# In the mixer's last tile, VectorE instead of GpSimd makes the low parts and the square sums

## The chip, the cores and the metric

The kernel runs on one core of one Trainium2 chip. The metric is the time of one execution on the device in microseconds; of several runs the median counts. Engines are named as the profile names them: PE is TensorE's matmuls, PEld its weight loads, DVE is VectorE, ACT is ScalarE, POOL is GpSimd, SP issues the DMA transfers. "Granted clock" is TensorE's clock as a share of 2.4 GHz; 0.50 is 1.2 GHz.

## The reference, cut to what matters

Eight sequences of 256 tokens with 256 features go through a layer norm. Its result feeds a state-space mixer and a six-block MLP, and the output is the input plus both results. The mixer:

```python
zxbcdt = hidden_states @ W_in
z, xbc, dt = ...
xbc = _causal_conv1d(xbc, conv_w, conv_b)
x, Bm, Cm = ...
dt = jax.nn.softplus(dt + dt_bias)
y = _ssd(x, dt, A, Bm, Cm, CHUNK)
y = y + D[None, None, :, None] * x
yg = y * _silu(z)
rms = jax.lax.rsqrt(jnp.mean(yg * yg, axis=-1, keepdims=True) + EPS)
yn = (yg * rms) * norm_w
return yn @ W_out
```

Two parts of it matter here: the gated result `yg`, which is multiplied by `W_out`, and the mean of its squares over all 4096 inner features.

## The kernel before, in words

The program has three phases with a barrier of all engines between them: `prepare` (layer norm, the projections of B, C and dt, decay sums), `mix` (the mixer) and `mlp` (the six blocks). All 2048 tokens stay in SBUF.

`mix` goes over the 4096 inner features in `NCT` = 32 tiles of 128 features (c = 0 to 31), and in each tile over `NB` = 4 blocks of 512 tokens (b = 0 to 3; two sequences s to a block). Matrix products are made in split precision: an operand is cut into a high part (a cast to fp32r on ScalarE) and a low part (operand minus high part), and three products are added. For the gated result of a tile and block the chain is:

1. VectorE makes the decay exponents (`exponents`, L989), ScalarE their exponential (`decays`, L874), GpSimd multiplies by masked C.B (`times_g`, L681), and TensorE multiplies with the tokens (`outputs`, L769) into one of two PSUM tensors `py`.
2. VectorE adds D.x (`add_dx`, L1004) and gates with silu(z) into `yg` (`gate`, L1017).
3. ScalarE squares it (`square`, L883) and casts the high part `ghi` (`high`, L919). GpSimd makes the low part `glo` (`low`, L670) and adds the square to the running sum `sqacc` (`add_square`, L690).
4. After every second tile TensorE multiplies the pair's `ghi` and `glo` with two tiles of `W_out` (`output_rows`, L787 to L789): eight groups of 12 matmuls, two groups to a block (i = 0, 1), each into one of two PSUM banks `po[i]`. VectorE adds each group to `acc` (`add_rows`, L1030), which frees the bank.

The order on each engine is written out by hand in its `step(c)`, which runs for c = -2 to 34 and is fully unrolled. One step works on several tiles at once: in step c GpSimd makes the products of tile c and the low parts and squares of tile c - 1. Engines run their lists in order, and semaphores that count upwards join them. The end of the mixer is step 32, where no tile of exponents is left, and the rest of the output rows in steps 33 and 34. In this text m0 to m7 are the eight groups of output rows of the last pair of tiles: m0 to m3 of step 32, m4 to m7 of step 33.

Group m waits until the addition of group m - 2 has emptied its bank:

```python
wait_past(pe, o_added, 2 * NB * q + 2 * b + i - 1)
```

On VectorE the end of the mixer is, in order: `gate` of block 2, `add_dx` of block 3, `add_rows` of the pair before, `add_rows` of m0, `gate` of block 3, `add_rows` of m1 to m7. On ScalarE `high` of blocks 2 and 3 stands behind `square` of block 3. After the output rows TensorE sums `sqacc` over the features with 16 one-column products (L822), VectorE makes the mean square from them (L1069), and the barrier ends the phase.

At the start of the mixer VectorE fills a PSUM tensor `floor` with a constant (L972); only its first column is read, by `exponents`, as a broadcast operand.

Of the kernel before, what the change touches and what calls it, by code (L numbers as in the profile page):

```python
# [23 lines left out]
F32 = mybir.dt.float32  # L24
F32R = mybir.dt.float32r
ALU = mybir.AluOpType
# [10 lines left out]
NCT = DI // P  # L37
PAIRS = NCT // 2
# [5 lines left out]
NB = TOK // BLK  # L44
TPB = BLK // P
SPB = BLK // SEQ
# [6 lines left out]
CAP = 80.0  # L53
# [468 lines left out]
def wait_past(eng, sem, count):  # L522

    if not (isinstance(count, int) and count <= 0):
        eng.wait_ge(sem, count)
# [6 lines left out]
def mix(nc, w_xz, conv_par, d_par, w_out, w1, cs_dram, ident, xhi, xlo, acc, gmat, tokpar,  # L532
        wraw, whi, wlo, w_in, conv, conv_in, srow, srow_in, xt, zt, stages, w1raw, w1_in, meansq):

    DVE_G = [(0, 0)]
    POOL_G = [(b, s) for b in range(NB) for s in range(SPB) if (b, s) not in DVE_G]

    with ExitStack() as ctx:
        sb = lambda name, shape, dt=F32: ctx.enter_context(nc.sbuf_tensor("mix_" + name, shape, dt))
        ps = lambda name: ctx.enter_context(nc.psum_tensor("mix_" + name, [P, BLK], F32))
# [39 lines left out]
        o_hi_done = sem("o_hi_done")  # L588
        o_split = sem("o_split")
        sq_added = sem("sq_added")  # L590
        o_done = sem("o_done")
        o_added = sem("o_added")
        pool_set = sem("pool_set")
# [4 lines left out]
        def tile_of(c):  # L598
            return Tile(c, c % 2, c // 2)
# [6 lines left out]
        def cols(b):  # L606
            return slice(b * BLK, (b + 1) * BLK)
# [33 lines left out]
        @block.gpsimd  # L641
        def _(pool):
            pool.memset(sqacc[:], 0.0).then_inc(pool_set, 1)
            pool.memset(onesq[:], 1.0).then_inc(pool_set, 1)
            pool.wait_ge(pool_set, 2)

            def w_lo(c):
                if not 2 <= c < NCT:
                    return
                t = tile_of(c)  # L650


                pool.wait_ge(w_hi_done, t.c - 1)
                pool.tensor_tensor(wlo[:, t.par].rearrange("p k m -> p (k m)"), wraw[:, t.par],
                                   whi[:, t.par].rearrange("p k m -> p (k m)").bitcast(F32),
                                   ALU.subtract).then_inc(w_split, 1)

            def o_lo(c):
                if c < 0 or c >= NCT or c % 2 == 0:
                    return  # L660
                pool.wait_ge(o_hi_done, c // 2 + 1)
                pool.tensor_tensor(olo[:], oraw[:, :, 0:DM], ohi[:].bitcast(F32),
                                   ALU.subtract).then_inc(o_split, 1)

            def low(c, b):
                if not 0 <= c < NCT:
                    return
                t = tile_of(c)
                pool.wait_ge(ghi_done, NB * t.c + b + 1)
                pool.tensor_tensor(glo[:, t.par, cols(b)], yg[:, b, :],  # L670
                                   ghi[:, t.par, cols(b)].bitcast(F32),
                                   ALU.subtract).then_inc(glo_done, 1)

            def times_g(c, b, s):
                if not 0 <= c < NCT:
                    return
                t = tile_of(c)
                pool.wait_ge(dec_done, SPB * (NB * t.c + b) + s + 1)
                d = dec[:, b % 2, s]
                g = gmat[:, b * SPB + s, :].unsqueeze(1).broadcast_to([P, HPT, LW])  # L680
                pool.tensor_tensor(d, d, g, ALU.mult).then_inc(g_done, 1)  # L681

            def add_square(c, b):
                if not 0 <= c < NCT:
                    return
                t = tile_of(c)
                n = NB * t.c + b
                pool.wait_ge(sq_done, n + 1)
                wait_past(pool, sq_added, n - NB + 1)
                pool.tensor_tensor(sqacc[:, cols(b)], sqacc[:, cols(b)], sq[:, b % 2, :],  # L690
                                   ALU.add).then_inc(sq_added, 1)

            def step(c):
                add_square(c - 1, 0)
                low(c - 1, 0)
                times_g(c, 0, 0)
                low(c - 1, 1)
                times_g(c, 0, 1)
                times_g(c, 1, 0)
                add_square(c - 1, 1)  # L700
                times_g(c, 1, 1)
                times_g(c, 2, 0)
                times_g(c, 2, 1)
                o_lo(c)
                w_lo(c + 2)
                add_square(c - 1, 2)
                low(c - 1, 2)
                times_g(c, 3, 0)
                add_square(c - 1, 3)
                times_g(c, 3, 1)  # L710
                low(c - 1, 3)

            steps(step)

        @block.tensor
        def _(pe):
# [56 lines left out]
            def output_rows(c, k):  # L773
                if not 2 <= c < NCT + 2:
                    return

                q, b, i = c // 2 - 1, 2 * (c % 2) + k // 2, k % 2

                if i == 0:
                    pe.wait_ge(glo_done, NB * (2 * q + 1) + b + 1)  # L780
                    pe.wait_ge(o_split, q + 1)
                wait_past(pe, o_added, 2 * NB * q + 2 * b + i - 1)
                for t in (2 * i, 2 * i + 1):
                    dst = po[i][:, (t % 2) * DM:(t % 2 + 1) * DM]
                    r = slice((b * TPB + t) * P, (b * TPB + t + 1) * P)
                    for e in range(2):
                        pe.matmul(dst, ghi[:, e, r], ohi[:, e, :], start=(e == 0), stop=False)  # L787
                        pe.matmul(dst, ghi[:, e, r], olo[:, e, :], start=False, stop=False)
                        last = pe.matmul(dst, glo[:, e, r], ohi[:, e, :], start=False, stop=(e == 1))  # L789
                last.then_inc(o_done, 1)  # L790
# [26 lines left out]

            steps(step)

            pe.wait_ge(sq_added, NB * NCT)  # L820
            for t in range(TILES):
                last = pe.matmul(pt[:, t:t + 1], sqacc[:, t * P:(t + 1) * P], onesq[:, 0:1],  # L822
                                 start=True, stop=True)
# [3 lines left out]
        def _(act):  # L827
# [48 lines left out]
            def square(c, b):  # L876
                if not 0 <= c < NCT:
                    return
                t = tile_of(c)
                n = NB * t.c + b  # L880
                act.wait_ge(gated, n + 1)
                wait_past(act, sq_added, n - 1)
                act.activation(sq[:, b % 2, :], yg[:, b, :], ACT.Square).then_inc(sq_done, 1)  # L883

            def copy_tokens(c, b):
# [75 lines left out]
        def _(dve):  # L961
            def tap(c, b, k):
                if not 1 <= c < NCT:
                    return
                t = tile_of(c)
                before, done = [(conv0_done, tap1_done), (tap1_done, tap2_done),
                                (tap2_done, conv_done)][k - 1]
                dve.wait_ge(before, NB * t.c + b + 1)
                conv_tap(dve, xt[:, t.par, cols(b)], pa[b % 2][:],
                         conv[:, t.par, TAPS - 1 - k:TAPS - k], k).then_inc(done, 1)  # L970

            dve.memset(floor[:], -CAP).then_inc(floor_set, 1)  # L972
            dve.wait_ge(floor_set, 1)

            def exponents(c, b, s):
# [31 lines left out]
            def gate(c, b):  # L1007
                if not 0 <= c < NCT:
# [8 lines left out]
                dve.tensor_tensor(yg[:, b, :], py[b % 2][:], zt[:, t.par, cols(b)],  # L1017
                                  ALU.mult).then_inc(gated, 1)

            def add_rows(c, k):  # L1020
                if not 2 <= c < NCT + 2:
                    return

                q, b, i = c // 2 - 1, 2 * (c % 2) + k // 2, k % 2
                m = 2 * NB * q + 2 * b + i
                dve.wait_ge(o_done, m + 1)

                wait_past(dve, o_added, m - 2 * NB + 1)
                rows = acc[:, b * TPB + 2 * i:b * TPB + 2 * i + 2, :].rearrange("p t d -> p (t d)")
                dve.tensor_tensor(rows, po[i][:], rows, ALU.add).then_inc(o_added, 1)  # L1030

            def step(c):
                gate(c - 1, 2)
                add_dx(c - 1, 3)
                exponents(c, 1, 1)
                tap(c + 1, 0, 1)
                add_rows(c - 1, 3)
                tap(c + 1, 1, 1)
                add_rows(c, 0)
                tap(c + 1, 0, 2)  # L1040
                tap(c + 1, 1, 2)
                tap(c + 1, 0, 3)
                tap(c + 1, 1, 3)
                gate(c - 1, 3)
                exponents(c, 2, 0)
                exponents(c, 2, 1)
                add_rows(c, 1)
                exponents(c, 3, 0)
                tap(c + 1, 2, 1)
                add_dx(c, 0)  # L1050
                tap(c + 1, 2, 2)
                gate(c, 0)
                exponents(c, 3, 1)
                tap(c + 1, 3, 1)
                tap(c + 1, 2, 3)
                tap(c + 1, 3, 2)
                tap(c + 1, 3, 3)
                add_dx(c, 1)
                exponents(c + 1, 0, 0)
                gate(c, 1)  # L1060
                add_rows(c, 2)
                add_dx(c, 2)
                exponents(c + 1, 0, 1)
                exponents(c + 1, 1, 0)
# [495 lines left out]
```

## Time and profile before

| | |
|---|---|
| median of 3 runs | 1522.66 us (1520.12 to 1525.63) |
| the profiled execution's own time | 1524.01 us |
| its span, first to last instruction | 1522.2 us |
| granted TensorE clock, mean over the span | 0.985 |
| busy share of the span: PE, DVE, POOL, ACT | 95%, 82%, 74%, 71% |
| mixer | from about 74.5 us to the barrier near 947.5 us |
| MLP | from there to the end |

The profiled execution's time is the span plus what lies around it. Busy shares are means over phases with different limits, so the rows below are taken from the stretches that the change touches. A timeline row gives the start, the time from the first start to the last end of the instructions merged in the row, the engine, line, operation and tile, the count, and in brackets how long the engine had been idle before and what released it.

### The profile page before, as it was taken

The numbers are of one execution on the slowest core, as the hardware profiler recorded it, in microseconds if no ns is written. First come the engines' busy times: TensorE is split into PE (matmuls) and PEld (weight loads), VectorE is DVE, ScalarE is ACT, GpSimd is POOL, SyncE is SP. The second block draws the span as 40 slices with busy tenths as digits, with TensorE's granted clock in tenths as the row PEclk, the third lists the DMA queues.
The fourth block names the chain that finished last, engine by engine and source line by source line (L and its number), as shares of the span: only waits on it lengthen the run. The fifth ranks groups of instructions, "written<-read, shape, count | busy, mean of one in ns | idle before, by whom it ended". The sixth has DMA issues, their size and how long they took to land. (4 is left out here: it accounts for less than half of the span.)

```text
span 1522.2 us, 27373 instructions
## 1 busy us (share of the span) xinstructions
PE 1448.4 (95%) x9432; PEld 1188.4 (78%) x9432; DVE 1255.7 (82%) x2534; ACT 1087.8 (71%) x1764; POOL 1119.7 (74%) x763
## 2 busy tenths in 40 slices
PE   6789999999999999999999997999999999999998
PEld 5556777777777777777777776899998989989988
DVE  6899999999999999999999993567666776776752
ACT  5679888888988888898888883656555555655542
POOL 4279999999999999999999997645263451634650
PEclk9899999999999999999999997999999999999999
DMA  4233323232332323232232210300101001020011
GB/s 142 72 130 105 97 79 105 83 105 91 105 98 74 102 90 105 91 105 98 70 100 96 98 56 26 128 1 29 39 2 66 0 28 38 0 79 0 1 56 42
DMA packets 50159, 107.62 MB, mean 71 GB/s; under 512 B 13248, under 2 KB 25792, under 8 KB 48448
## 3 DMA queue, kind: packets, MB, share of 16 engines
q1 hardware_dynamic: 50048, 106.21, 21.3%
q8 instruction: 61, 1.00, 0.3%
q14 instruction: 50, 0.41, 0.1%
HBM read 101.47 MB, written 4.72 MB: 70 GB/s over the span
## 5 line engine op out<-in xcount | busy, mean ns | idle before, releaser
L681 POOL TENSOR_TENSOR mix_dec<-mix_dec,gmat 128x768 f32<-128x768 f32 x256 | 471.1, 1862 | 17.1 <-ACT mix_dec L874 17.1
L1411 DVE TENSOR_TENSOR mlp_hlo<-mlp_h,mlp_hhi 128x512 fp32r<-128x512 f32 x192 | 209.6, 1093 | 181.9 <-ACT mlp_hhi L1343 181.5
L989 DVE SCALAR_TENSOR_TENSOR mix_dec<-srow,tokpar,mix_floor 128x256 f32<-128x256 f32 (+1 forms) x1024 | 348.9, 408 | 11.9 <-PE mix_py L769 11.9
L1338 ACT ACTIVATE mlp_h<-mlp_p,mlp_b1c 128x512 f32<-128x512 f32 x192 | 132.1, 688 | 203.4 <-PE mlp_p L501 197.5
L517 DVE SCALAR_TENSOR_TENSOR xt<-mix_pa,conv,xt 128x510 f32<-128x510 f32 x372 | 262.3, 740 | 12.3 <-ACT xt L847 9.6
L501 PE MATMUL mix_pa<-xhi,whi 128*128 128x512 f32 x496 | 212.8, 429 | 20.5 <-DVE xt L517 19.6
L769 PE MATMUL mix_py<-mix_dec,mix_xtok 128*64 128x256 f32 (+1 forms) x2048 | 215.0, 339 | 15.9 <-ACT mix_xtok L892 8.6
L1304 PE MATMUL mlp_p<-mlp_w2hi,mlp_hhi 128*128 128x256 f32 x768 | 218.6, 285 | 3.2 <-DVE acc L1470 3.2
L1306 PE MATMUL mlp_p<-mlp_w2hi,mlp_hlo 128*128 128x256 f32 x768 | 216.5, 282 | 0.0
L769 PEld LDWEIGHTS mix_py<-mix_dec,mix_xtok 128*64 128x64 f32 x2048 | 128.4, 137 | 112.2 <-issue 57.8
L1305 PE MATMUL mlp_p<-mlp_w2lo,mlp_hhi 128*128 128x256 f32 x768 | 216.0, 281 | 0.0
L874 ACT ACTIVATE mix_dec<-mix_dec 128x768 f32<-128x768 f32 x256 | 212.9, 844 | 3.8 <-DVE mix_dec L989 2.8
L501 PE MATMUL mix_pa<-xlo,whi 128*128 128x512 f32 x496 | 196.7, 397 | 0.0
L501 PE MATMUL mix_pa<-xhi,wlo 128*128 128x512 f32 x496 | 196.6, 396 | 0.0
L690 POOL TENSOR_TENSOR mix_sqacc<-mix_sqacc,mix_sq 128x512 f32<-128x512 f32 x128 | 166.6, 1302 | 4.5 <-ACT mix_sq L883 4.5
L670 POOL TENSOR_TENSOR mix_glo<-mix_yg,mix_ghi 128x512 fp32r<-128x512 f32 x128 | 167.4, 1308 | 1.9 <-ACT mix_ghi L919 1.9
L501 PE MATMUL mlp_p<-xhi,mlp_w1hi 128*128 128x512 f32 x384 | 153.5, 400 | 2.0 <-POOL mlp_w1lo L1199 2.0
L1304 PEld LDWEIGHTS mlp_p<-mlp_w2hi,mlp_hhi 128*128 128x128 f32 x768 | 144.6, 188 | 13.4 <-DVE mlp_hlo L1411 3.6
L501 PE MATMUL mlp_p<-xlo,mlp_w1hi 128*128 128x512 f32 x384 | 153.3, 399 | 0.0
L501 PE MATMUL mlp_p<-xhi,mlp_w1lo 128*128 128x512 f32 x384 | 153.2, 399 | 0.0
L787 PE MATMUL mix_po<-mix_ohi,mix_ghi 128*128 128x256 f32 x512 | 148.6, 290 | 3.5 <-POOL mix_glo L670 2.1
L1305 PEld LDWEIGHTS mlp_p<-mlp_w2lo,mlp_hhi 128*128 128x128 f32 x768 | 144.6, 188 | 6.1
(130 smaller groups left out, 3207.8 us busy)
## 6 DMA issues: line engine op xcount, KB each, us to landing
srow<-cs_rows SPq DMA_DIRECT2D x128, 512.0 KB, 4.6
wraw<-w_xz SPq DMA_DIRECT2D x32, 256.0 KB, 5.6
w1raw<-w SPq DMA_DIRECT2D x6, 1028.0 KB, 4.8
mlp_w2raw<-w SPq DMA_DIRECT2D x6, 1024.0 KB, 6.7
mix_oraw<-w_out SPq DMA_DIRECT2D x16, 257.0 KB, 5.5
prep_hid<-hidden SPq DMA_DIRECT2D x4, 512.0 KB, 6.6
xn_rows<-prep_hid SPq DMA_DIRECT2D x4, 512.0 KB, 2.9
mlp_res<-xn_rows SPq DMA_DIRECT2D x1, 2048.0 KB, 10.2
```

Of the source, the lines that this page charges most:

```text
L501: last = pe.matmul(dst, w[:, k, :], x[:, k, cols], start=(i == 0), stop=(i == len(passes) - 1))
L517: return dve.scalar_tensor_tensor(d[:, :, k:SEQ], s[:, :, 0:SEQ - k], weight, d[:, :, k:SEQ], ALU.mult, ALU.add)
L670: pool.tensor_tensor(glo[:, t.par, cols(b)], yg[:, b, :], ghi[:, t.par, cols(b)].bitcast(F32), ALU.subtract).then_inc(glo_done, 1)
L681: pool.tensor_tensor(d, d, g, ALU.mult).then_inc(g_done, 1)
L690: pool.tensor_tensor(sqacc[:, cols(b)], sqacc[:, cols(b)], sq[:, b % 2, :], ALU.add).then_inc(sq_added, 1)
L769: last = pe.matmul(py[b % 2][hp, i], xtok[:, b % 2, 2 * s + j, hp], dec[:, b % 2, s, h, m], start=(j == 0), stop=(j == 1))
L874: act.activation(d, d, ACT.Exp, scale=-1.0).then_inc(dec_done, 1)
L989: last = dve.scalar_tensor_tensor(dec[:, b % 2, s, h, k], srow[:, half, h, i], tokpar[:, tile, HPT * c + h:HPT * c + h + 1], floor[:, 0:1] ...
L1304: pe.matmul(dst, hhi[:, j, k], w2hi[:, j, :], start=(j == 0), stop=False)
L1305: pe.matmul(dst, hhi[:, j, k], w2lo[:, j, :], start=False, stop=False)
L1306: last = pe.matmul(dst, hlo[:, j, k], w2hi[:, j, :], start=False, stop=(j == KH - 1))
L1411: dve.tensor_tensor(hlo[:, j, :], h[:, j % 4, :], hhi[:, j, :].bitcast(F32), ALU.subtract).then_inc(hlo_done, 1)
```

## The change

For the last tile alone (c = 31) the low parts and the additions to the square sum move from GpSimd to VectorE, in a new function `last_parts(c, b)`; GpSimd keeps both for the other 31 tiles and the products by masked C.B for all. Two new semaphores count the moved operations: TensorE's output rows of the last pair wait for the last tile's low parts on `last_glo_done`, ScalarE's squares of blocks 2 and 3 and TensorE's mean-square matmuls wait on `last_sq_added`. In VectorE's step `last_parts` of blocks 0 and 1 stands behind `add_rows(c - 1, 3)`, that of blocks 2 and 3 behind `gate(c - 1, 3)`. Besides, the fill of `floor` shrinks to its first column, and two unused lists go.

```diff
@@ gpsimd
             def low(c, b):
-                if not 0 <= c < NCT:
+                if not 0 <= c < NCT - 1:
                     return
@@
             def add_square(c, b):
-                if not 0 <= c < NCT:
+                if not 0 <= c < NCT - 1:
                     return
@@ tensor, output_rows
                 if i == 0:
-                    pe.wait_ge(glo_done, NB * (2 * q + 1) + b + 1)
+                    if q < PAIRS - 1:
+                        pe.wait_ge(glo_done, NB * (2 * q + 1) + b + 1)
+                    else:
+                        pe.wait_ge(glo_done, NB * (NCT - 1))
+                        pe.wait_ge(last_glo_done, b + 1)
@@ tensor, after the steps
-            pe.wait_ge(sq_added, NB * NCT)
+            pe.wait_ge(last_sq_added, NB)
@@ scalar, square
-                wait_past(act, sq_added, n - 1)
+                if c == NCT - 1 and b >= 2:
+                    act.wait_ge(last_sq_added, b - 1)
+                else:
+                    wait_past(act, sq_added, n - 1)
@@ vector
-            dve.memset(floor[:], -CAP).then_inc(floor_set, 1)
+            dve.memset(floor[:, 0:1], -CAP).then_inc(floor_set, 1)
@@
+            def last_parts(c, b):
+
+                if c != NCT - 1:
+                    return
+                t = tile_of(c)
+                dve.wait_ge(ghi_done, NB * c + b + 1)
+                dve.tensor_tensor(glo[:, t.par, cols(b)], yg[:, b, :],
+                                  ghi[:, t.par, cols(b)].bitcast(F32),
+                                  ALU.subtract).then_inc(last_glo_done, 1)
+                dve.wait_ge(sq_done, NB * c + b + 1)
+                dve.wait_ge(sq_added, NB * (c - 1) + b + 1)
+                dve.tensor_tensor(sqacc[:, cols(b)], sqacc[:, cols(b)], sq[:, b % 2, :],
+                                  ALU.add).then_inc(last_sq_added, 1)
@@ vector, step
                 add_rows(c - 1, 3)
+                last_parts(c - 1, 0)
+                last_parts(c - 1, 1)
                 tap(c + 1, 1, 1)
                 add_rows(c, 0)
...
                 gate(c - 1, 3)
+                last_parts(c - 1, 2)
+                last_parts(c - 1, 3)
                 exponents(c, 2, 0)
                 exponents(c, 2, 1)
                 add_rows(c, 1)
```

VectorE's order at the end of the mixer before, from the D.x addition of the last tile's block 3 to the mean square. `mix_py` is the tensor of the D.x addition, `mix_yg` the gate, and `acc<-mix_po` a row addition (the first of the x2 belongs to the pair before, the second is m0, the x7 are m1 to m7):

```order
L1004 SCALAR_TENSOR_TENSOR mix_py<-xt,mix_dcol,mix_py 128x512 [waits mix_y_done]
L1030 TENSOR_TENSOR acc<-mix_po,acc 128x512 [waits mix_o_added,mix_o_done] x2
L1017 TENSOR_TENSOR mix_yg<-mix_py,zt 128x512 [waits mix_sq_done,mix_glo_done,z_done,mix_yd_done]
L1030 TENSOR_TENSOR acc<-mix_po,acc 128x512 [waits mix_o_added,mix_o_done] x7
L1069 TENSOR_SCALAR meansq<-mix_pt 128x16 [waits mix_ms_done]
```

The same place in the changed kernel, from the row addition of the pair before:

```order
L1042 TENSOR_TENSOR acc<-mix_po,acc 128x512 [waits mix_o_added,mix_o_done]
L1024 TENSOR_TENSOR mix_glo<-mix_yg,mix_ghi 128x512 [waits mix_ghi_done]
L1029 TENSOR_TENSOR mix_sqacc<-mix_sqacc,mix_sq 128x512 [waits mix_sq_added,mix_sq_done]
L1024 TENSOR_TENSOR mix_glo<-mix_yg,mix_ghi 128x512 [waits mix_ghi_done]
L1029 TENSOR_TENSOR mix_sqacc<-mix_sqacc,mix_sq 128x512 [waits mix_sq_added,mix_sq_done]
L1042 TENSOR_TENSOR acc<-mix_po,acc 128x512 [waits mix_o_added,mix_o_done]
L1015 TENSOR_TENSOR mix_yg<-mix_py,zt 128x512 [waits mix_sq_done,mix_glo_done,z_done,mix_yd_done]
L1024 TENSOR_TENSOR mix_glo<-mix_yg,mix_ghi 128x512 [waits mix_ghi_done]
L1029 TENSOR_TENSOR mix_sqacc<-mix_sqacc,mix_sq 128x512 [waits mix_sq_added,mix_sq_done]
L1024 TENSOR_TENSOR mix_glo<-mix_yg,mix_ghi 128x512 [waits mix_ghi_done]
L1029 TENSOR_TENSOR mix_sqacc<-mix_sqacc,mix_sq 128x512 [waits mix_sq_added,mix_sq_done]
L1042 TENSOR_TENSOR acc<-mix_po,acc 128x512 [waits mix_o_added,mix_o_done] x7
```

The four moved operations of blocks 0 and 1 stand between the row addition of the pair before and that of m0; the four of blocks 2 and 3 stand between the gate of block 3 and the row additions of m1 to m7.

GpSimd's order at the end of the mixer before; `mix_dec` is a product by masked C.B, `mix_glo` a low part, `mix_sqacc` a square sum:

```order
L681 TENSOR_TENSOR mix_dec<-mix_dec,gmat 128x768 [waits mix_dec_done]
L670 TENSOR_TENSOR mix_glo<-mix_yg,mix_ghi 128x512 [waits mix_ghi_done]
L690 TENSOR_TENSOR mix_sqacc<-mix_sqacc,mix_sq 128x512 [waits mix_sq_added,mix_sq_done]
L670 TENSOR_TENSOR mix_glo<-mix_yg,mix_ghi 128x512 [waits mix_ghi_done] x2
L690 TENSOR_TENSOR mix_sqacc<-mix_sqacc,mix_sq 128x512 [waits mix_sq_added,mix_sq_done] x2
L670 TENSOR_TENSOR mix_glo<-mix_yg,mix_ghi 128x512 [waits mix_ghi_done]
L690 TENSOR_TENSOR mix_sqacc<-mix_sqacc,mix_sq 128x512 [waits mix_sq_added,mix_sq_done]
L670 TENSOR_TENSOR mix_glo<-mix_yg,mix_ghi 128x512 [waits mix_ghi_done]
L546 UNCONDITIONAL_BRANCH
```

The same place in the changed kernel:

```order
L672 TENSOR_TENSOR mix_dec<-mix_dec,gmat 128x768 [waits mix_dec_done]
L681 TENSOR_TENSOR mix_sqacc<-mix_sqacc,mix_sq 128x512 [waits mix_sq_added,mix_sq_done]
L672 TENSOR_TENSOR mix_dec<-mix_dec,gmat 128x768 [waits mix_dec_done]
L661 TENSOR_TENSOR mix_glo<-mix_yg,mix_ghi 128x512 [waits mix_ghi_done]
L535 UNCONDITIONAL_BRANCH
```

The last product and the low part of tile 30's block 3 now end GpSimd's list; the eight operations of tile 31 behind them are gone, and the branch out of the phase follows.

## Rows read from the trace of the kernel before

**Rows 1.** The page's head.

```profile
span 1522.2 us, 27373 instructions
```

**Rows 2.** Stretches: length; busy PE, PEld, DVE, ACT, POOL; granted clock; DMA.

```profile
877.00:904.00 27.00, 26.34 (x186) 20.44 (x183) 26.39 (x59) 23.19 (x38) 25.05 (x17) 1.00 0.24 79
...
931.00:934.00 3.00, 3.00 (x16) 3.00 (x16) 1.29 (x2) 0.21 (x1) 2.15 (x2) 0.50 0.00 0
...
937.00:940.00 3.00, 3.00 (x27) 3.00 (x26) 1.45 (x3) 0.00 (x0) 1.81 (x2) 1.00 0.00 0
```

**Rows 3.** Timeline of POOL at the mixer's end.

```profile
923.97 1.81 POOL L681 TENSOR_TENSOR mix_dec<-mix_dec,gmat 128x768 f32<-128x768 f32 x1
...
926.95 1.27 POOL L690 TENSOR_TENSOR mix_sqacc<-mix_sqacc,mix_sq 128x512 f32<-128x512 f32 x1
928.17 2.50 POOL L670 TENSOR_TENSOR mix_glo<-mix_yg,mix_ghi 128x512 fp32r<-128x512 f32 x2
...
935.01 1.29 POOL L670 TENSOR_TENSOR mix_glo<-mix_yg,mix_ghi 128x512 fp32r<-128x512 f32 x1 [1.85 <-ACT mix_ghi L919]
...
937.50 1.31 POOL L670 TENSOR_TENSOR mix_glo<-mix_yg,mix_ghi 128x512 fp32r<-128x512 f32 x1
```

**Rows 4.** Timeline of DVE at the mixer's end.

```profile
927.43 0.76 DVE L1004 SCALAR_TENSOR_TENSOR mix_py<-xt,mix_dcol,mix_py 128x512 f32<-128x512 f32 x1 [5.57 <-PE mix_py L769]
928.09 0.68 DVE L1030 TENSOR_TENSOR acc<-mix_po,acc 128x512 f32<-128x512 f32 x1
932.47 0.69 DVE L1030 TENSOR_TENSOR acc<-mix_po,acc 128x512 f32<-128x512 f32 x1 [3.69 <-PE mix_po L789]
933.08 0.68 DVE L1017 TENSOR_TENSOR mix_yg<-mix_py,zt 128x512 f32<-128x512 f32 x1
934.94 0.69 DVE L1030 TENSOR_TENSOR acc<-mix_po,acc 128x512 f32<-128x512 f32 x1 [1.18 <-PE mix_po L789]
```

**Rows 5.** Timeline of ACT at the mixer's end and the MLP's start.

```profile
933.79 0.63 ACT L883 ACTIVATE mix_sq<-mix_yg 128x512 f32<-128x512 f32 x1 [4.85 <-DVE mix_yg L1017]
934.33 1.12 ACT L919 CAST mix_ghi<-mix_yg 128x512 fp32r<-128x512 f32 x2
947.50 0.20 ACT L1360 COPY mlp_b1c<-w1raw 128x8 f32<-128x8 f32 x1 [12.05 <-PEq L546]
```

**Rows 6.** Timeline of PE: last products, m0's first, m1's last, m3's first, mean square.

```profile
925.83 1.55 PE L769 MATMUL mix_py<-mix_dec,mix_xtok 128*64 128x256 f32 x8 [1.35 <-POOL mix_dec L681]
929.50 0.58 PE L787 MATMUL mix_po<-mix_ohi,mix_ghi 128*128 128x256 f32 x1 [2.12 <-POOL mix_glo L670]
...
934.58 0.33 PE L789 MATMUL mix_po<-mix_ohi,mix_glo 128*128 128x256 f32 x1
...
936.17 0.28 PE L787 MATMUL mix_po<-mix_ohi,mix_ghi 128*128 128x256 f32 x1
...
943.37 3.63 PE L822 MATMUL mix_pt<-mix_onesq,mix_sqacc 128*128 128x1 f32 x32
```

**Rows 7.** MLP's low part on DVE: ns min/median/max; then timelines of DVE, POOL.

```profile
L1411 DVE TENSOR_TENSOR mlp_hlo<-mlp_h,mlp_hhi x192: 677/693/2891, 954.7 to 1507.4; 128x512 fp32r<-128x512 f32 x192
...
971.06 10.53 DVE L1411 TENSOR_TENSOR mlp_hlo<-mlp_h,mlp_hhi 128x512 fp32r<-128x512 f32 x5 [4.87 <-ACT mlp_hhi L1343]
...
969.62 10.82 POOL L1235 TENSOR_TENSOR mlp_res<-mlp_res,mlp_grow 128x1024 f32<-128x1024 f32 x4
```

**Rows 8.** Timeline of DVE: the mixer's first operations, and its last.

```profile
74.50 0.48 DVE L972 MEMSET mix_floor<- 128x512 f32 x1 [3.31 <-PEq L114]
75.02 5.29 DVE L989 SCALAR_TENSOR_TENSOR mix_dec<-srow,tokpar,mix_floor 128x256 f32<-128x256 f32 x16
...
947.04 0.17 DVE L1069 TENSOR_SCALAR meansq<-mix_pt 128x16 f32<-128x16 f32 x1 [2.78 <-PE mix_pt L822]
```

**Rows 9.** Early mixer: timeline of PE, and a stretch (columns of rows 2).

```profile
107.31 1.74 PE L769 MATMUL mix_py<-mix_dec,mix_xtok 128*64 128x256 f32 x16 [2.81 <-ACT mix_xtok L892]
...
109.00:109.50 0.50, 0.50 (x5) 0.50 (x4) 0.50 (x2) 0.04 (x1) 0.50 (x1) 0.50 0.00 0
```

More of the change, by code:

```diff
@@ L533, in mix @@
         wraw, whi, wlo, w_in, conv, conv_in, srow, srow_in, xt, zt, stages, w1raw, w1_in, meansq):
-    DVE_G = [(0, 0)]
-    POOL_G = [(b, s) for b in range(NB) for s in range(SPB) if (b, s) not in DVE_G]
     with ExitStack() as ctx:
@@ L590, in mix @@
         sq_added = sem("sq_added")
+        last_glo_done = sem("last_glo_done")
+        last_sq_added = sem("last_sq_added")
         o_done = sem("o_done")
```

## Prediction

> **What bounds the kernel now.** I read the page's head first: the profiled span is 1522.2 us [rows 1], and that execution took 1524.01 us, so 1.8 us lie around the span. Then I read the stretches by busy time: in a steady mixer step TensorE, VectorE and GpSimd are all busy for over 26 of 27 us [rows 2]. The change doesn't touch those steps. It touches the step after the last tile's exponents, so I read that end engine by engine, in order of time.
>
> GpSimd: the last product by masked C.B starts at 923.97 and is followed by the previous tile's last low part. Only then come the last tile's eight operations. They start with the square sum of block 0 at 926.95, go on with the first low part at 928.17 (two in 2.50, so the first ends near 929.44), and end with the last low part, started at 937.50 [rows 3].
>
> VectorE: it waits 5.57 us for TensorE until 927.43, when it adds D.x for block 3. After that it mostly waits for TensorE's output rows [rows 4].
>
> ScalarE: the high parts of blocks 2 and 3 start only at 934.33, as they stand behind the square of block 3, which needs the gate of block 3 that VectorE finished just before [rows 5].
>
> TensorE: the output rows come in eight groups of 12 matmuls, m0 to m7 (two per block, alternating between two PSUM banks). m0 starts at 929.50, after 2.12 us of waiting for GpSimd's first low part; m1 ends about 934.7; m3 starts at 936.17; the mean-square matmuls follow at 943.37 [rows 6]. From m3 on, 60 matmuls take 7.20 us, 0.120 each, at a granted clock of 1.00 (2.4 GHz); while m0 and m1 ran it was 0.50 (1.2 GHz) [rows 2]. **So TensorE's output rows end the mixer**: ScalarE's next work, at 947.50, waits for TensorE through the barrier between the phases [rows 5]. What comes later on TensorE moves the end of the program one for one.
>
> **The change, part by part.**
>
> *The memset.* VectorE's fill of the floor shrinks from 128x512 to 128x1. Before, it took 0.48 at 74.50 and the exponents followed back to back from 75.02 for 5.29 us [rows 8]. No row shows a 128x1 fill; the nearest small operation is the mean square's 128x16 at 0.17 [rows 8], which makes the saving up to 0.31. It could be 0 if another engine sets the pace of the first steps. I take the middle, -0.2.
>
> *The removal on GpSimd.* Eight operations of about 1.25 go. All of them stand behind its last products, so no product comes earlier. GpSimd has nothing else until the next phase, whose first operation waits for ScalarE. Worth 0 by itself.
>
> *Blocks 0 and 1 on VectorE.* The four new operations stand behind the D.x addition at 927.43 and the row addition at 928.09 [rows 4]. One VectorE operation of 128x512 starts 0.61 after another (932.47 to 933.08 [rows 4]) and lasts 0.69. That is also the usual duration of the nearest operation with two SBUF inputs, the MLP's low part at 0.693 [rows 7]. So the first low part runs from 928.70 to 929.39, against GpSimd's 929.44, and m0 starts 0.05 earlier. The other three end by 931.2, inside the 3.69 us that VectorE idled before 932.47 [rows 4]: hidden. Without that cover they would delay the gate of block 3, and with it everything below. ScalarE's square of block 2 now waits for VectorE's first sum (930.0, not 928.2) and is not needed before 935.
>
> *Blocks 2 and 3 on VectorE.* This is the term that counts. Both pairs stand between the gate of block 3 (933.08) and the row addition of m1, which before ran at 934.94 [rows 4]. Their first operation needs ScalarE's high part of block 2: two casts from 934.33 in 1.12, the first done at 934.93 [rows 5]. VectorE is in order, so the addition of m1 can't pass. Low part of block 2 at 934.97, then one each 0.61: sum at 935.58, low part of block 3 at 936.19, sum at 936.80, addition of m1 at 937.41, done at 938.10. TensorE's m3 writes the bank that this addition empties; with the 0.05 from a release to a matmul it starts at 938.15 instead of 936.17 [rows 6]: **+1.98**. Below, it can't fall far: casts and order are fixed, and even at one operation fewer it is +1.4. Above, if the four don't overlap and each costs 0.69 and 0.05 of release, they take 2.96 instead of 2.44: +2.5. Then the pipe catches up: m2's addition follows at 938.02, and the later groups at 1.44 each need one every 1.44.
>
> *The last wait.* The mean-square matmuls now wait for VectorE's fourth sum, done at 937.5; they come at about 945.35. Worth 0.
>
> Sum: -0.2 - 0.05 + 1.98 = +1.7 us, or 1525.7 on the profiled execution. That execution lies 1.35 above the median of the runs shown (1522.66), so I forecast **1524.4** for the median.
>
> **A rule against the change.** In the MLP five low parts on VectorE took 10.53 us, 2.1 each, and the longest of all 2.891, while GpSimd's residual additions ran from 969.62 for 10.82; alone they take 0.69 [rows 7]. So such an operation is three times as dear beside GpSimd. The Trainium skill (SBUF — State Buffer, "Who interferes with whom") says why: a VectorE instruction with two SBUF inputs shares a read path with a GpSimd instruction that reads SBUF, and the later one waits until the other is through. By that rule alone VectorE is a poor home for these eight operations; the trace agrees in the MLP's rows. In the changed kernel GpSimd's last mixer work is the low part that ends before 927.0 [rows 3], and VectorE's first new operation is at 928.70, so the sum goes by 0.69.
>
> **Rivals.**
>
> *Port contention (the other side, slower than 0.3%).* Place: VectorE's new operations, if GpSimd still worked when they came. Price: the four late ones at 2.1 instead of 0.61 add 4 x 1.5 = 6 to the +1.7: 1530.4. It decides only if GpSimd's last mixer operation slips by 1.7 us relative to VectorE. Against it: VectorE waits for matmuls that themselves wait for GpSimd's last product, so the order is nearly forced. Chance 0.05.
>
> *TensorE's clock falls in the new gap.* TensorE now idles about 1.8 us before m3. In the second mixer step a gap of 2.81 us before 107.31 was followed by 1.7 us of matmuls, and at 109.00 the granted clock was 0.50 [rows 9]. So a fall is possible after a gap only half again as long. Price: m0 and m1, 24 matmuls at 0.50, took 5.2 us where 24 at 0.120 take 2.9: 2.4 more. Total +4.1: 1526.8. Against it: matmuls stand densely on both sides of this gap. [...] The trace has one gap that speaks for it. Chance 0.15.
>
> *No stall, or a gain.* If the additions of m1 and m2 weren't on TensorE's path, or the low part of block 0 came as soon as VectorE had nothing else, the wait of 2.12 before m0 could shrink: at most 1522.66 - 2.1 = 1520.5, at least no change, 1522.5. Against it: the order puts two VectorE operations ahead of that low part. Chance 0.17. That the change does nothing at all is not open: the new waits are in the order.
>
> **How the numbers follow.** The forecast has 0.63. A measurement of this kernel can tell about 0.3%, 4.6 us, from no change. Its own bounds, +1.1 to +2.5, and the scatter of the runs shown (1520.12 to 1525.63), which a median of three doesn't remove wholly, give 1522.3 to 1526.3. For 8 in 10 I add the clock's fall on one end and the no-stall case on the other: 1521.0 to 1528.0. Faster by over 0.3%: 0.03, from the last rival at its best plus scatter. Slower by over 0.3%: 0.05 from contention and 0.06 from a longer stretch at the low clock: 0.11. Within: 0.86.
>
> **What would show it.** Right: m0 starts within 0.2 of 929.5 counted from the same matmuls; VectorE's row addition of m1 starts behind four new operations; TensorE has a gap of about 1.8 between m2 and m3, released by that addition; the barrier comes 1.5 to 2 later. Wrong: new operations of over 1 us each; a granted clock of 0.50 after m3; no gap before m3; or a mixer whose steady steps, which the change leaves alone, take another time.

## The result, and the profile after

The changed kernel takes 1525.09 us (median of 20 runs, 1523.40 to 1528.69), the kernel before 1522.37 (median of 20 runs beside them, 1520.12 to 1525.63). The ratio is 1.0020, with a 95% interval of 1.0013 to 1.0027: the change costs 2.0 to 4.1 us. The profiled execution of the changed kernel took 1525.72 us, with a span of 1523.7: 2.02 us lie around the span, where it was 1.81 before.

VectorE at the mixer's end, timeline of the changed kernel (start, us, engine, line, operation, what it waited for):

```profile
927.20 0.76 DVE L1002 SCALAR_TENSOR_TENSOR mix_py<-xt,mix_dcol,mix_py 128x512 f32<-128x512 f32 x1 [5.58 <-PE mix_py L760]
927.87 0.68 DVE L1042 TENSOR_TENSOR acc<-mix_po,acc 128x512 f32<-128x512 f32 x1
928.47 0.68 DVE L1024 TENSOR_TENSOR mix_glo<-mix_yg,mix_ghi 128x512 fp32r<-128x512 f32 x1
...
932.19 0.69 DVE L1042 TENSOR_TENSOR acc<-mix_po,acc 128x512 f32<-128x512 f32 x1 [1.24 <-PE mix_po L784]
932.80 0.68 DVE L1015 TENSOR_TENSOR mix_yg<-mix_py,zt 128x512 f32<-128x512 f32 x1
934.69 0.69 DVE L1024 TENSOR_TENSOR mix_glo<-mix_yg,mix_ghi 128x512 fp32r<-128x512 f32 x1 [1.20 <-ACT mix_ghi L917]
935.29 0.69 DVE L1029 TENSOR_TENSOR mix_sqacc<-mix_sqacc,mix_sq 128x512 f32<-128x512 f32 x1
935.90 0.68 DVE L1024 TENSOR_TENSOR mix_glo<-mix_yg,mix_ghi 128x512 fp32r<-128x512 f32 x1
936.50 0.69 DVE L1029 TENSOR_TENSOR mix_sqacc<-mix_sqacc,mix_sq 128x512 f32<-128x512 f32 x1
937.10 1.28 DVE L1042 TENSOR_TENSOR acc<-mix_po,acc 128x512 f32<-128x512 f32 x2
```

Against [rows 4]: behind the gate (932.80) VectorE now waits 1.20 us for ScalarE's high part, then does the four moved operations, and only at 937.10 adds m1, whose last matmul had ended at 934.71. In the kernel before that addition came 1.86 behind the gate (934.94 after 933.08), now it comes 4.30 behind it.

TensorE there, timeline of the changed kernel (m0's first matmul, m1's last, m2's last before the gap, m3's first, the mean square):

```profile
929.25 0.55 PE L782 MATMUL mix_po<-mix_ohi,mix_ghi 128*128 128x256 f32 x1 [2.10 <-issue]
...
934.30 0.41 PE L784 MATMUL mix_po<-mix_ohi,mix_glo 128*128 128x256 f32 x1
...
936.19 0.28 PE L784 MATMUL mix_po<-mix_ohi,mix_glo 128*128 128x256 f32 x1
937.84 0.38 PE L782 MATMUL mix_po<-mix_ohi,mix_ghi 128*128 128x256 f32 x1 [1.37 <-DVE acc L1042]
...
945.13 3.63 PE L817 MATMUL mix_pt<-mix_onesq,mix_sqacc 128*128 128x1 f32 x32
```

In the kernel before m3 (936.17 in [rows 6]) followed m2 without a pause, as its last matmul had started at 936.05:

```profile
936.05 0.28 PE L789 MATMUL mix_po<-mix_ohi,mix_glo 128*128 128x256 f32 x1
```

In the changed kernel m3 waits 1.37 us, and the row names VectorE's row addition as what ended the wait. From m0's first matmul to the mean square it is 15.88 us instead of 13.87: +2.01.

Two stretches of the changed kernel (columns of [rows 2]):

```profile
931.00:934.00 3.00, 3.00 (x16) 3.00 (x16) 1.29 (x2) 0.48 (x1) 0.00 (x0) 0.50 0.00 0
...
937.00:940.00 3.00, 2.16 (x18) 2.16 (x19) 1.82 (x4) 0.00 (x0) 0.00 (x0) 1.00 0.00 0
```

GpSimd is idle in both (0.00, where [rows 2] had 2.15 and 1.81), and the clock behind this gap is 1.00. GpSimd's last operation of the mixer ends at 926.78, ahead of VectorE's first new one (928.47):

```profile
925.47 1.31 POOL L661 TENSOR_TENSOR mix_glo<-mix_yg,mix_ghi 128x512 fp32r<-128x512 f32 x1
```

ScalarE and the start of the next phase, timelines of the changed kernel:

```profile
929.85 0.63 ACT L881 ACTIVATE mix_sq<-mix_yg 128x512 f32<-128x512 f32 x1 [5.33 <-DVE mix_sqacc L1029]
...
934.05 1.12 ACT L917 CAST mix_ghi<-mix_yg 128x512 fp32r<-128x512 f32 x2
949.26 0.20 ACT L1376 COPY mlp_b1c<-w1raw 128x8 f32<-128x8 f32 x1 [14.09 <-PEq L535]
```

The square of block 2 waits for VectorE's first sum, and nothing suffers from it. The barrier comes at 949.26 instead of 947.50 [rows 5], 1.76 later; counted from m0 it is the same 2.01 later, as m0 started 0.25 sooner in this execution.

The start of the mixer, timeline of VectorE in the changed kernel:

```profile
74.86 0.06 DVE L970 MEMSET mix_floor<- 128x1 f32 x1 [3.19 <-PEq L114]
74.95 5.29 DVE L987 SCALAR_TENSOR_TENSOR mix_dec<-srow,tokpar,mix_floor 128x256 f32<-128x256 f32 x16
```

The short fill takes 0.06, and the exponents start 0.09 behind its start, where it was 0.52 [rows 8].

### The profile page after: what moved, and what is told of

Its sections match the earlier page's. It is cut to its first block and busy times, and to the rows that moved or that the text cites. A ratio compares the mean times of both kernels' runs of the same rounds, so it can differ in the third digit from the quotient of the medians.

```text
span 1523.7 us, 27377 instructions
## 1 busy us (share of the span) xinstructions
PE 1447.8 (95%) x9432; PEld 1187.8 (78%) x9432; DVE 1262.4 (83%) x2542; ACT 1087.6 (71%) x1764; POOL 1109.9 (73%) x755
## 5 line engine op out<-in xcount | busy, mean ns | idle before, releaser
L1427 DVE TENSOR_TENSOR mlp_hlo<-mlp_h,mlp_hhi 128x512 fp32r<-128x512 f32 x192 | 212.9, 1111 | 180.4 <-ACT mlp_hhi L1359 180.0
L681 POOL TENSOR_TENSOR mix_sqacc<-mix_sqacc,mix_sq 128x512 f32<-128x512 f32 x124 | 161.2, 1300 | 4.8 <-ACT mix_sq L881 4.8
L661 POOL TENSOR_TENSOR mix_glo<-mix_yg,mix_ghi 128x512 fp32r<-128x512 f32 x124 | 161.8, 1305 | 0.0
```

Source lines behind the costliest of these rows:

```text
L661: pool.tensor_tensor(glo[:, t.par, cols(b)], yg[:, b, :], ghi[:, t.par, cols(b)].bitcast(F32), ALU.subtract).then_inc(glo_done, 1)
L1427: dve.tensor_tensor(hlo[:, j, :], h[:, j % 4, :], hhi[:, j, :].bitcast(F32), ALU.subtract).then_inc(hlo_done, 1)
```

## The experiments

The theory: the four operations of blocks 2 and 3 hold back m1's row addition, TensorE's m3 waits for the bank, and everything behind it is late. The rivals: the operations are dear on VectorE wherever they stand, blocks 0 and 1 or ScalarE's changed waits carry the loss, or the clock does. All ratios are to the kernel before, run beside the experiment on the same chip.

**Parts by need.** `last_parts` is cut in two, `last_low` and `last_sum`, and the late ones are moved (the last place belongs to the next step, where the row addition is that of m3):

```diff
                 gate(c - 1, 3)
-                last_parts(c - 1, 2)
-                last_parts(c - 1, 3)
...
                 add_rows(c, 1)
+                last_low(c - 1, 2)
...
                 add_rows(c, 2)
+                last_low(c - 1, 3)
...
                 add_rows(c - 1, 3)
...
+                last_sum(c - 2, 2)
+                last_sum(c - 2, 3)
```

> The change with the same eight operations on VectorE, but the four of blocks 2 and 3 put where they are needed: the low part of block 2 behind m1's row addition, that of block 3 behind m2's, both sums behind m3's. Theory (the four operations ahead of m1's addition make TensorE wait before m3): no gap before m3, from m0's first matmul to the first mean-square matmul 13.9 us as before instead of 15.9, the time 1.5 to 2.5 below the changed kernel and within 1 us of the kernel before. Rival (the operations are dear on VectorE wherever they stand, or the new waits of ScalarE's squares cost): the stretch stays near 15.9 and the time at 1.002 of before.

Measured: 1522.08 us, ratio 0.9999 (0.9988 to 1.0011). At this place the same eight operations cost nothing that can be told from the scatter. From m0 to the mean square it was 14.28 us instead of the 13.9 expected, without a gap: the clock rose only in the middle of m2 there. VectorE's timeline in this kernel:

```profile
931.21 0.68 DVE L1015 TENSOR_TENSOR mix_yg<-mix_py,zt 128x512 f32<-128x512 f32 x1
933.17 0.69 DVE L1045 TENSOR_TENSOR acc<-mix_po,acc 128x512 f32<-128x512 f32 x1 [1.27 <-PE mix_po L784]
933.77 0.68 DVE L1023 TENSOR_TENSOR mix_glo<-mix_yg,mix_ghi 128x512 fp32r<-128x512 f32 x1
934.91 0.69 DVE L1045 TENSOR_TENSOR acc<-mix_po,acc 128x512 f32<-128x512 f32 x1 [0.45 <-PE mix_po L784]
935.52 0.68 DVE L1023 TENSOR_TENSOR mix_glo<-mix_yg,mix_ghi 128x512 fp32r<-128x512 f32 x1
```

Now it is VectorE that waits for TensorE (1.27, 0.45), each low part fits between two row additions, and there is no gap before m3. Both rivals are out, operations that are dear on VectorE wherever they stand and ScalarE's new waits: this kernel has them all.

**Only blocks 0 and 1 on VectorE.** The guards in `low` and `add_square` let GpSimd keep blocks 2 and 3, and the waits count accordingly:

```diff
-                if not 0 <= c < NCT - 1:
+                if not 0 <= c < NCT or (c == NCT - 1 and b < 2):
...
-                last_parts(c - 1, 2)
-                last_parts(c - 1, 3)
```

> Half the change: only blocks 0 and 1 of the last tile on VectorE, blocks 2 and 3 back on GpSimd. Theory: no gap before m3, 13.9 us from m0 to the mean-square matmuls, the time within 1 us of the kernel before, since the first four operations lie in VectorE's idle time. Rival (blocks 0 and 1 carry the loss, by delaying the gate of block 3 or ScalarE's square of block 2): over 15 us and about 1.002 of before.

Measured: 1521.46 us, ratio 0.9993 (0.9981 to 1.0006); 13.68 us from m0 to the mean square, no gap. Blocks 0 and 1 cost nothing that can be told, as forecast.

**Six operations ahead.** The sums of blocks 0 and 1 are put behind the gate of block 3 as well:

```diff
                 add_rows(c - 1, 3)
-                last_parts(c - 1, 0)
-                last_parts(c - 1, 1)
+                last_low(c - 1, 0)
+                last_low(c - 1, 1)
...
                 gate(c - 1, 3)
-                last_parts(c - 1, 2)
-                last_parts(c - 1, 3)
+                last_sum(c - 1, 0)
+                last_sum(c - 1, 1)
+                last_low(c - 1, 2)
+                last_sum(c - 1, 2)
+                last_low(c - 1, 3)
+                last_sum(c - 1, 3)
```

> The suspected cost made larger: the two sums of blocks 0 and 1 are put behind the gate of block 3 too, so that six operations stand ahead of m1's row addition, and the squares of blocks 2 and 3 wait for them. Theory: m1's addition 1.2 us later than in the changed kernel, a gap before m3 of about 2.6 instead of 1.4 us idle, 17.1 us from m0 to the mean-square matmuls, the time about 1.2 above the changed kernel (1526.3 if that is at 1525.1). Rival (the clock, not the stall, makes the loss): the stretch grows by other than 1.2, with a granted clock of 0.50 behind the gap. Rival (no stall): no difference from the changed kernel.

Measured: 1527.95 us, ratio 1.0033 (1.0023 to 1.0044). From m0 to the mean square 17.15 us, within 0.05 of what the theory said; VectorE's first late low part and m3's row on TensorE in this kernel:

```profile
934.24 0.69 DVE L1023 TENSOR_TENSOR mix_glo<-mix_yg,mix_ghi 128x512 fp32r<-128x512 f32 x1 [1.27 <-ACT mix_ghi L917]
```

```profile
937.39 0.39 PE L782 MATMUL mix_po<-mix_ohi,mix_ghi 128*128 128x256 f32 x1 [3.05 <-DVE acc L1045]
```

So the stall follows what stands ahead of m1's addition. The two sums act through ScalarE too: its squares wait for them, its high parts come later, and VectorE again waits 1.27 us for the first. The idle time is 3.05 and not 2.6, since the clock rose sooner, at the end of m1, and m2 was through sooner. But the time rose by 5.5 us over the kernel before instead of the 4 expected, and the stretch in this one execution only by 3.3. That left 2 us open, and in the changed kernel 0.7. Both kernels were profiled once more for the clock, without any edit:

> A second look at the kernel with six operations ahead of m1's addition, for the clock behind the gap. In 12 runs it lay 5.5 us above the kernel before by the medians, while its profiled execution had only 3.3 us more from m0 to the mean square, at a granted clock of 1.00 behind the gap. Theory: in a part of the executions the clock falls behind the gap, to 0.50 for some us, and the stretch is then about 2 us longer (19 instead of 17.15). Rival: the stretch is 17.15 again, whatever the execution's time, and the rest of the loss lies elsewhere.

> The changed kernel once more, for the same reason: by the medians it lost 2.7 us, its profiled execution showed 2.0 more from m0 to the mean square. Theory: m3 waits for m1's row addition again (1.3 to 1.9 us idle) whatever the clock does; if the clock falls behind the gap, the stretch is 1.5 to 2 longer than 15.9. Rival: a stretch near 13.9, the gap having been an accident of one execution.

The kernel with six operations ahead (1528.98 us in this execution), row of m3 and two stretches:

```profile
939.19 0.58 PE L782 MATMUL mix_po<-mix_ohi,mix_ghi 128*128 128x256 f32 x1 [2.94 <-DVE acc L1045]
```

```profile
937.00:938.00 1.00, 0.00 (x0) 0.00 (x0) 1.00 (x3) 0.00 (x0) 0.00 (x0) 1.00 0.00 0
938.50:939.00 0.50, 0.00 (x0) 0.00 (x0) 0.50 (x2) 0.00 (x0) 0.00 (x0) 0.50 0.00 0
940.00:942.00 2.00, 2.00 (x11) 2.00 (x11) 0.00 (x0) 0.00 (x0) 0.00 (x0) 0.50 0.00 0
```

Here the clock fell to 0.50 (1.2 GHz) while TensorE waited, m3 and m4 ran at half rate (11 matmuls in 2 us), and the stretch was 19.68 us, 2.5 more than in the first execution. The changed kernel showed 15.89 and no fall there; that this execution took 1527.57 us came later, for the most part in the MLP (574.4 us from its first matmul to the end, 572.9 in the first profile). Three more executions of it:

> The changed kernel again, first of three looks at the clock behind its gap. In two profiled executions m3 waited for m1's row addition and the clock stayed at 1.00 behind the gap (15.88 and 15.89 us from m0 to the mean square); the kernel with six operations showed it falling once in two, with a stretch 2.5 us longer. Theory (the clock adds to the loss in some executions of the change too): in at least one of the three looks the clock is at 0.50 behind m3's start and the stretch 17 to 18.5. Rival (a gap of 1.4 to 1.9 us is too short for a fall): 15.8 to 16 in all three.

> Second of the three looks, as the first: 17 to 18.5 us from m0 to the mean square with the clock at 0.50 behind the gap in at least one of the three by the theory, 15.8 to 16 in all by the rival.

> Third of the three looks, as the first: 17 to 18.5 us from m0 to the mean square with the clock at 0.50 behind the gap in at least one of the three by the theory, 15.8 to 16 in all by the rival.

15.88, 17.37 and 15.88 us. In the second of them the clock fell behind the gap; row of m3 and two stretches of that execution:

```profile
936.26 0.38 PE L782 MATMUL mix_po<-mix_ohi,mix_ghi 128*128 128x256 f32 x1 [2.81 <-DVE acc L1042]
```

```profile
936.00:938.00 2.00, 1.74 (x12) 1.74 (x13) 0.80 (x2) 0.00 (x0) 0.00 (x0) 0.83 0.00 0
938.00:940.00 2.00, 2.00 (x11) 2.00 (x11) 0.69 (x1) 0.00 (x0) 0.00 (x0) 0.50 0.00 0
```

In that execution the clock had risen sooner, so m1 ran at full rate and TensorE waited 2.81 us instead of 1.3 to 1.7. m3 began at full rate, and about 1 us into it the clock fell.

The stretch ends too early to show all of it. The clock fell once more in that execution, within the mean-square matmuls, which took 4.54 us where the first profile had 3.63; the execution of 15.89 us shows the same at 4.03. Row and stretch of the first, row of the second:

```profile
945.04 4.54 PE L817 MATMUL mix_pt<-mix_onesq,mix_sqacc 128*128 128x1 f32 x32
```

```profile
948.00:949.00 1.00, 1.00 (x6) 1.00 (x6) 0.00 (x0) 0.00 (x0) 0.00 (x0) 0.50 0.00 0
```

```profile
945.10 4.03 PE L817 MATMUL mix_pt<-mix_onesq,mix_sqacc 128*128 128x1 f32 x32
```

They take 3.93 us in the third execution of the change and 4.30 in the second one with six operations ahead; in no execution without a gap do they take over 3.63. So the table counts on to the MLP's first matmul. The starts of m3, from m0's first matmul, are the telling numbers:

| execution | m3 behind m0 | idle before m3 | m0 to mean square | m0 to the MLP's first matmul |
|---|---|---|---|---|
| kernel before | 6.67 | none | 13.87 | 19.49 |
| only the short fill | 6.41 | none | 13.61 | 19.24 |
| only blocks 0 and 1 | 6.48 | none | 13.68 | 19.31 |
| parts by need | 7.05 | none | 14.28 | 19.90 |
| the change, five executions | 8.59, 8.58, 8.59, 8.59, 8.59 | 1.37, 1.71, 1.67, 2.81, 1.33 | 15.88, 15.89, 15.88, 17.37, 15.88 | 21.51, 21.91, 21.81, 23.90, 21.51 |
| six operations ahead, two | 9.85, 9.85 | 3.05, 2.94 | 17.15, 19.68 | 22.77, 25.97 |

With the change m3 starts 8.59 us behind m0 whenever the clock rises after m0: in all five executions m0 ran at half rate, and from m0's row addition on VectorE and ScalarE set the start. Without the change it comes when m2 is through, sooner where the clock rises sooner. Counted to the MLP's first matmul, the mean of the five executions of the change (22.13 us) lies 2.8 above that of the three kernels that leave blocks 2 and 3 on GpSimd (19.35), and the mean of the two with six operations ahead (24.37) lies 5.0 above it.

**The short fill alone**, in the kernel before:

```diff
-            dve.memset(floor[:], -CAP).then_inc(floor_set, 1)
+            dve.memset(floor[:, 0:1], -CAP).then_inc(floor_set, 1)
```

> The kernel before with nothing but the short fill of the floor. Theory: the first exponents start 0.4 us sooner behind the barrier, 0.09 instead of 0.52 behind the fill's start; the time 0 to 0.4 below the kernel before, too little for the rounds to tell. Rival (the fill hides in another engine's wait): the steady steps start no sooner, same time. A loss of 0.7 or more here would explain why the changed kernel lost more than the stall's 2.0.

Measured: 1521.84 us, ratio 0.9998 (0.9986 to 1.0009). The exponents start 0.09 behind the fill's start, as in the changed kernel. What of the 0.43 reaches the end can't be told: from the fill to m0 it is 855.00 us in the kernel before, 854.66 here, and 854.36 to 854.89 in the five executions of the change. No loss of 0.7 shows, though the interval's upper end, 1.4 us, would hold one.

**Early parts.** If VectorE is to help, m0 should not wait for a low part at all. The low parts of blocks 0 and 1 go into VectorE's idle 5.6 us, with the row addition of the pair before ahead of them; the gate of block 3 goes ahead of m0's addition, and the late parts stay by need:

```diff
                 gate(c - 1, 2)
+                if c == NCT:
+                    add_rows(c - 1, 3)
+                last_low(c - 1, 0)
+                last_low(c - 1, 1)
                 add_dx(c - 1, 3)
+                if c == NCT:
+                    gate(c - 1, 3)
+                last_sum(c - 1, 0)
+                last_sum(c - 1, 1)
...
```

> The eight operations on VectorE, put by need at both ends: the low parts of blocks 0 and 1 right behind the gate of block 2, in the 5.6 us in which VectorE waits for the last products, the gate of block 3 ahead of m0's row addition, the late parts as in the version by need. Theory (GpSimd's last low part was what m0 waited for, 2.1 us): m0 starts within 0.1 to 0.6 us of the last output matmuls instead of 2.1, the stretch from m0 stays at 13.9, the time about 2 us below the kernel before (1520.5 if that is at 1522.5). Rival (port contention): the two early low parts run beside GpSimd's last products, take 1 to 2.5 us instead of 0.68 or make GpSimd's product of 1.8 us longer, and the last output matmuls come up to 1.4 us later, so that 0.5 to 1.5 of the 2 are given back.

A second version adds a wait for GpSimd's last product ahead of the two low parts:

```diff
+                if c == NCT:
+                    dve.wait_ge(g_done, SPB * NB * NCT)
                 last_low(c - 1, 0)
```

> As the early version, but VectorE's two early low parts wait until GpSimd's last product by masked C.B is done, so that only the previous tile's last low part on GpSimd (1.3 us) can run beside them. If contention costs the early version something, here the last product comes no later than in the kernel before, the first low part is held up behind GpSimd's at most 1.3 us, and m0 starts 0.2 to 0.6 us behind the last output matmul: 1.5 to 2 us below the kernel before. If there is no contention, it is equal to the early version or up to 0.3 slower.

Measured: 1520.08 us, ratio 0.9989 (0.9977 to 1.0001), and 1520.16 us, ratio 0.9984 (0.9974 to 0.9994). The second version's interval lies below 1, while the change's lies above it, so it beats both kernels; the first one's just reaches 1, and the two versions can't be told apart. Their stretch from m0 is 13.02 and 13.25 us instead of the 13.9 expected, since the clock rose earlier behind m0. The early version's VectorE, GpSimd and TensorE, timelines:

```profile
920.59 5.18 DVE L1023 TENSOR_TENSOR mix_glo<-mix_yg,mix_ghi 128x512 fp32r<-128x512 f32 x1
```

```profile
920.97 1.27 POOL L681 TENSOR_TENSOR mix_sqacc<-mix_sqacc,mix_sq 128x512 f32<-128x512 f32 x1
922.19 1.80 POOL L672 TENSOR_TENSOR mix_dec<-mix_dec,gmat 128x768 f32<-128x768 f32 x1
923.95 1.27 POOL L661 TENSOR_TENSOR mix_glo<-mix_yg,mix_ghi 128x512 fp32r<-128x512 f32 x1
```

```profile
924.05 1.55 PE L760 MATMUL mix_py<-mix_dec,mix_xtok 128*64 128x256 f32 x8 [1.34 <-POOL mix_dec L672]
925.87 0.56 PE L782 MATMUL mix_po<-mix_ohi,mix_ghi 128*128 128x256 f32 x1 [0.27 <-issue]
```

m0 now waits 0.27 instead of 2.12 [rows 6], and starts 1.82 behind the start of the last output matmuls instead of 3.67. VectorE's first low part took 5.18 us instead of 0.68: it began at 920.59 and ended at 925.77, 0.55 behind the end of GpSimd's last operation (925.22). GpSimd's own times are unchanged (1.80 for a product, 1.81 in [rows 3]). So contention is there and large, but it costs at most the 0.27 that m0 still waits, because the low part comes 0.17 behind the end of the last products on TensorE (925.60). The rival's half that GpSimd would be slowed fell.

In the second version the first low part starts when GpSimd has only its last operation left, and ends at 926.95, again 0.55 behind that one's end (926.40); m0 waits 0.27 there too:

```profile
925.21 1.74 DVE L1023 TENSOR_TENSOR mix_glo<-mix_yg,mix_ghi 128x512 fp32r<-128x512 f32 x1 [3.36 <-POOL mix_dec L672]
```

```profile
925.12 1.28 POOL L661 TENSOR_TENSOR mix_glo<-mix_yg,mix_ghi 128x512 fp32r<-128x512 f32 x1
```

## Why the prediction was right, and what it mis-sized

- *What bounds the kernel.* Right where it counts: TensorE's output rows end the mixer, and what delays m3 comes through to the barrier and to the time. Two readings on the way are off, and the sum doesn't use them: in a steady step GpSimd is busy for 25.05 of 27 us, not over 26 [rows 2], and m1 ends at 934.91 (934.58 + 0.33), not about 934.7 [rows 6].
- *Blocks 2 and 3, "+1.98".* Right, and shown by removing it (parts by need, only blocks 0 and 1: nothing lost) and enlarging it (17.15 where 17.1 was expected). In the profiled execution it was +2.01 from m0 to the mean square. The assumed 0.05 from a release to a matmul came out (addition done at 937.79, m3 at 937.84).
- *Blocks 0 and 1: hidden, m0 0.05 earlier.* Right within what can be seen: m0 started 3.64 us behind the start of the last output matmuls (929.25 after 925.61), before 3.67.
- *The duration 0.69, starts 0.61 apart.* Right: 0.68 to 0.69, 0.60 to 0.61 apart.
- *The memset, "-0.2".* Its bound "up to 0.31" was too low: a 128x1 fill takes 0.06, so 0.43 are saved at that place. How much of that reaches the end stays open, and with it whether the -0.2 was right.
- *Port contention.* It did not decide in the changed kernel, as argued: GpSimd was through at 926.78, VectorE's first new operation came at 928.47. The price of 2.1 was a mean over unlike operations: of the five in [rows 7] the last ran behind GpSimd's work in 0.68, the four beside it took 1.51 to 2.89. Where VectorE's low part ran beside GpSimd in the mixer, it took 5.18 and 1.74. The Trainium skill (SBUF — State Buffer, "Who interferes with whom") says that a VectorE instruction with two SBUF inputs contends with a GpSimd instruction that reads SBUF, and that the one issued later is blocked while the other runs. The trace agrees in the 1.74; in the 5.18 VectorE was held by several in a row.
- *TensorE's clock falls in the gap.* This was weighed as a rival to the stall; it is an addition to it. Right behind the gap it fell in one of five executions of the change (+1.5 in the stretch, where the price was 2.4) and in one of two with six operations ahead (+2.5); a granted clock of 0.50 after m3 was a sign that the prediction had named for being wrong. The Trainium skill (TensorE: Matmul & The Clock Gate, "HAM oscillation — how this bites in real kernels") describes a kernel whose bursts of matmuls are broken by waits long enough for the clock to fall back to half. The trace agrees behind the waits of 2.94 and, about 1 us later, 2.81 us, and not behind the one of 3.05.
- *The clock in the mean-square matmuls.* This is in no term and no rival. In three of the five executions of the change the clock fell there and cost 0.3 to 0.9 us; in six executions without a gap it did not.
- *No stall, or a gain.* Not in the change. The gain that this rival names, from 2.1 us less of waiting before m0, is what the early parts got: 1520.08 us where it had 1520.5.

Forecast was a loss of 1.7 us, measured was 2.7 (2.0 to 4.1). The term that was sized too small is the stall. It was taken from one execution, in which the clock rose only at the end of m1. The start of m3 with the change is fixed by other engines, so an execution whose clock rises early gives that gain away, and may lose more by a fall of the clock behind the gap or in the mean-square matmuls. From m0 to the MLP's first matmul it measures 2.8 in the mean of the five executions, or 2.6 if the parts by need are counted with the three kernels that it is set against.

A second part lies where no row shows it. The prediction took the 1.8 us around the span as fixed. They are 1.8 in the runs of the kernel before, of the short fill and of blocks 0 and 1 alone (1.73 to 1.87), and 2.0 in the 20 runs of the change (1.89 to 2.14), as in all versions with the late parts on VectorE. What makes these 0.2 us is not shown.

The parts add up to the measured loss within its interval, but that is weak support: the MLP alone takes 570.7 to 574.4 us from execution to execution. That the gap brings the later fall of the clock is not shown either, and how often the clock falls was not measured closely.

## What to carry to other kernels

Before work is moved to a faster engine that runs in order, list what stands behind the new place, and ask for each whether another engine waits for it: here eight operations cost nothing or 2.7 us on VectorE, by their place alone. Put an operation that frees a buffer ahead of one that is needed only later. Then look for the wait that the faster engine could really shorten (here 2.1 us before m0), which lay at another place than the change.

## What the runs showed of the hardware

A VectorE operation with two SBUF inputs that began while GpSimd worked through a row of operations was held until 0.55 us behind the end of the last of them, 5.18 us instead of 0.68, and GpSimd lost nothing. That is not so everywhere. In the MLP of the kernel before [rows 7] such operations came through behind one GpSimd operation each, though the next had already begun, and GpSimd's took 2.85 us where the first took 2.40:

```profile
972.50 2.88 DVE L1411 TENSOR_TENSOR mlp_hlo<-mlp_h,mlp_hhi 128x512 fp32r<-128x512 f32 x1
```

```profile
971.98 2.85 POOL L1235 TENSOR_TENSOR mlp_res<-mlp_res,mlp_grow 128x1024 f32<-128x1024 f32 x1
974.79 2.85 POOL L1235 TENSOR_TENSOR mlp_res<-mlp_res,mlp_grow 128x1024 f32<-128x1024 f32 x1
```

What decides between the two cases is not shown.

Of waits on TensorE, one of 2.94 us ended with the clock at 1.2 GHz, one of 2.81 was followed by the fall about 1 us after its end, and one of 3.05 by none. So the length of a wait alone does not decide whether the clock falls; what else does is not shown.
